# Making the low parts of late q and k on GpSimd instead of VectorE in a self-attention kernel

## The reference

```python
# x (8, 512, 512), cond (8, 512); W* (512, 512), b* (512); 16 heads of 32
Q  = split_heads(x @ Wq.T + bq);     K  = split_heads(x @ Wk.T + bk);   V = split_heads(x @ Wv.T + bv)
tQ = split_heads(tokens @ Wq.T + bq);  tK = split_heads(tokens @ Wk.T + bk)      # tokens = cond[:, None, :]
scores = einsum('bhqd,bhkd->bhqk', Q + tQ, K + tK) / sqrt(32)
out = einsum('bhqk,bhkd->bhqd', softmax(scores), V)
return x + out.transpose(0, 2, 1, 3).reshape(8, 512, 512)
```

## Time and profile before

| | |
|---|---|
| median of 3 runs | 639.27 us (638.93 to 641.06) |
| the profiled execution | 639.64 us, of it the span 637.8 us |
| TensorE, weight loads | 631.6 us busy (99%), 441.0 us (69%) |
| VectorE, ScalarE, GpSimd | 542.4 us (85%), 390.2 us (61%), 490.2 us (77%) |

### The profile page before, as it was taken

One profiled execution on the slowest core, in us unless ns is written; L12 is line 12 of the kernel. 1 busy time (PEld: TensorE's weight loads), 2 busy tenths in 40 slices (PEclk: granted clock), 3 DMA queues, 4 the chain that ended last, 5 costly groups with the idle time before them and its releaser, 6 DMA issues.

```text
span 637.8 us, 10063 instructions
## 1 busy us (share of the span) xinstructions
PE 631.6 (99%) x3528; PEld 441.0 (69%) x3528; DVE 542.4 (85%) x818; ACT 390.2 (61%) x684; POOL 490.2 (77%) x204
## 2 busy tenths in 40 slices
PE   8999999999999999999999999999999999999997
PEld 6777677666677666776666776666776666876642
DVE  6886888888888888888888888888888889998697
ACT  6366567666566565666665666665676655555773
POOL 6448877778877788877788777788777787767993
PEclk9999999999999999999999999999999999999999
DMA  8944435555335564434564344554354556555201
GB/s 254 272 102 119 104 103 127 121 152 145 97 102 122 138 152 126 107 105 119 149 151 116 105 115 118 151 151 106 105 126 118 151 127 158 134 120 130 76 31 67
DMA packets 48243, 80.83 MB, mean 127 GB/s; under 512 B 9545, under 2 KB 9801, under 8 KB 48073
## 3 DMA queue, kind: packets, MB, share of 16 engines
q1 hardware_dynamic: 47837, 80.04, 48.7%
q10 hardware_dynamic: 356, 0.16, 0.1%
HBM read 19.95 MB, written 8.39 MB: 44 GB/s over the span
## 4 chain that ended last, share of the span: by engine, by line
PE 97%; DVE 1%; DMA 1%; SPq 0%; POOLq 0%; ACT 0%; issue 0%
PE bank L354 27%; PE bank L447 19%; PE bank L429 18%; PE bank L467 18%; PE bank L402 14%; DVE bank L751 1%; PE bank L498 1%; DMA Pt<-xT 1%; PE bank L475 0%; PE bank L379 0%; DVE Xl L720 0%; POOLq L82 0%; ACT Xh L594 0%; DVE rr L789 0%; DVE rr L800 0%
## 5 line engine op out<-in xcount | busy, mean ns | idle before, releaser
L647 ACT ACTIVATE Pt<-bank 128x512 f32<-128x512 f32 x512 | 301.0, 599 | 222.1 <-PE bank L447 156.7
L751 DVE TENSOR_REDUCE mf<-bank 128x1 f32<-128x512 f32 x496 | 330.9, 684 | 60.7 <-PE bank L429 59.7
L959 POOL TENSOR_TENSOR A<-A,Pt 128x2048 f32<-128x2048 f32 x59 | 271.3, 4598 | 4.6
L429 PE MATMUL bank<-Ks,Qs 128*128 128x512 f32 x496 | 194.3, 392 | 0.1
L447 PE MATMUL bank<-Qs,Ks 128*128 128x512 f32 x496 | 194.0, 398 | 0.3 <-DVE bank L751 0.3
L959 POOL TENSOR_TENSOR A<-Pt 128x2048 f32<-128x2048 f32 x30 | 138.4, 4612 | 25.5 <-DVE part_sums L776 22.1
L447 PEld LDWEIGHTS bank<-Qs,Ks 128*128 128x128 f32 x496 | 92.6, 188 | 46.9 <-ACT Pt L647 23.3
L467 PE MATMUL bank<-Pt,V 128*32 128x512 f32 x1024 | 119.0, 596 | 0.0
L429 PEld LDWEIGHTS bank<-Ks,Qs 128*128 128x128 f32 x496 | 93.0, 188 | 21.7 <-DVE bank L751 1.8
L354 PE MATMUL bank<-Xh,Wh 128*128 128x512 f32 x256 | 100.1, 391 | 0.4 <-ACT Xh L594 0.3
L354 PE MATMUL bank<-Xl,Wh 128*128 128x512 f32 x256 | 99.8, 390 | 0.3 <-DVE Xl L720 0.3
(11 more groups left out here) (74 smaller groups left out, 392.6 us busy)
## 6 DMA issues: line engine op xcount, KB each, us to landing
Qs<-hi SPq DMA_DIRECT2D x60, 256.0 KB
Ks<-hi SPq DMA_DIRECT2D x60, 256.0 KB, 4.0
Qs<-lo SPq DMA_DIRECT2D x30, 256.0 KB
Ks<-lo SPq DMA_DIRECT2D x30, 256.0 KB, 3.9
xr<-xT SPq DMA_DIRECT2D x28, 256.0 KB, 2.7
res<-xT SPq DMA_DIRECT2D x28, 256.0 KB, 2.9
outT<-ot SPq DMA_DIRECT2D x28, 256.0 KB, 3.6
Qs<-mt SPq DMA_DIRECT2D x122, 4.0 KB
```

What stands on the lines that cost most here:

```text
L429: e.matmul(MXB[u % 2][:, :], q[:, j, qc * P:(qc + 1) * P], k[:, j, :], start=True, stop=True).then_inc(t_mx, 1)
L647: e.activation(exponentials(g)[:, kc, j, :], st_bank(u)[:, :], ACT.Exp, scale=SCALE).then_inc(a_e, 1)
L751: e.reduce_max(to[:, 4 * j + qc:4 * j + qc + 1], MXB[u % 2][:, :], AXX).then_inc(v_mx, 1)
L959: e.tensor_tensor(sums, ex[:, 0, :, :] if kc == 1 else sums, ex[:, kc, :, :], ALU.add).then_inc(p_a, 1)
```

## The change

For groups 28 to 31, q and k, VectorE's `qk_lo` goes. ScalarE makes two activations of the bank: hi as before, and right behind it `whole`, bank + bias in float32, into a new buffer of 128 x 512 in SBUF, of which there is one. GpSimd subtracts hi from it (`qk_lo(i)` in the GpSimd program; i = 0 to 7 for q28, k28, q29 and so on) and signals p_lo. The bank is free in the ring after `whole` (a_f), the next `whole` may be written after GpSimd's subtraction of the one before (p_lo), and SP issues the copy of lo after p_lo. LATE_LO now gives, for each of the eight, a place in GpSimd's program: three places per group from group 25 on, ahead of `parts`, ahead of add(t, 1) and ahead of add(t, 2). By (1, 2, 3, 4, 6, 6, 8, 9), q28 stands ahead of add(25, 1), k28 ahead of add(25, 2), q29 ahead of parts(27), k29 ahead of add(26, 1), q30 and k30 ahead of parts(28), q31 ahead of add(27, 2) and k31 ahead of parts(29). The tables MAXIMA, LATE_PROJ and LATE_HI, a V copy, the value matmuls of group 28, the turn of the maxima of group 30 and the fourth score bank are placed anew.

```diff
--- before.py
+++ after.py
@@ -52,28 +52,28 @@
 
 
 EARLY = 7
-MAXIMA = ((1, 1, 1, 2, 1, 0, 2, 0, 1, 1, 1, 1, 2, 1, 0, 2),
-          (1, 1, 2, 1, 1, 1, 0, 2, 0, 2, 0, 2, 1, 1, 1, 1),
-          (1, 2, 2, 2, 0, 2, 0, 2, 0, 1, 1, 2, 1, 1, 1, 1),
-          (1, 1, 1, 1, 2, 0, 0, 1, 0, 2, 1, 1, 0, 2, 1, 1),
+MAXIMA = ((2, 0, 1, 2, 2, 0, 2, 0, 1, 1, 1, 1, 1, 1, 1, 2),
+          (1, 1, 2, 1, 1, 1, 0, 2, 0, 2, 0, 1, 1, 1, 2, 1),
+          (1, 1, 2, 2, 0, 2, 0, 2, 0, 1, 1, 2, 1, 1, 1, 1),
+          (1, 1, 1, 1, 2, 0, 0, 2, 0, 2, 1, 0, 1, 2, 1, 0),
           (1, 0, 1, 1, 1, 1, 1, 1, 0, 1, 1, 0, 1, 0, 0, 1),
           (1, 1, 0, 1, 1, 1, 0, 1, 1, 1, 0, 0, 0, 0, 0, 0))
 LATE = (("q", 28), ("k", 28), ("q", 29), ("k", 29), ("q", 30), ("k", 30), ("q", 31), ("k", 31),
         ("v", 28), ("v", 29), ("v", 30), ("v", 31))
-LATE_PROJ = ((1, 0, 3, 4, 4, 3, 3, 3, 0, 4, 1, 2, 3, 1, 2, 4),
-             (0, 0, 4, 0, 4, 4, 1, 5, 1, 3, 1, 3, 2, 1, 1, 1),
-             (2, 1, 5, 2, 4, 3, 2, 4, 4, 0, 3, 3, 1, 2, 1, 1),
-             (1, 0, 1, 2, 4, 1, 5, 3, 1, 3, 2, 1, 2, 3, 1, 1),
+LATE_PROJ = ((1, 1, 3, 4, 3, 3, 3, 1, 2, 4, 1, 2, 2, 1, 2, 4),
+             (0, 0, 5, 0, 5, 3, 0, 5, 1, 3, 1, 3, 2, 2, 3, 0),
+             (1, 0, 5, 1, 4, 4, 3, 4, 4, 1, 2, 3, 1, 2, 1, 2),
+             (0, 0, 1, 2, 4, 1, 5, 3, 0, 3, 2, 1, 2, 3, 1, 2),
              (1, 2, 1, 2, 0, 0, 0, 0, 0, 0, 0, 0, 0, 0, 0, 0))
-LATE_HI = ((4, 10), (15, 22), (31, 34), (39, 43))
-LATE_LO = ((5, 13), (16, 24), (32, 34), (40, 47))
-LATE_V = (50, 57, 67, 69)
-
-END_VALUES_AT = ((5, 13), (15,), (3, 7))
-END_TURN_AT = 5
+LATE_HI = ((4, 11), (16, 21), (27, 36), (39, 43))
+LATE_LO = (1, 2, 3, 4, 6, 6, 8, 9)
+LATE_V = (50, 57, 68, 69)
+
+END_VALUES_AT = ((5, 11), (15,), (3, 7))
+END_TURN_AT = 4
 END_SUMS_AT = 11
 POOL_ADDS = 2
-END_BANKS = ((1, 7, 3), (2, 12, 4))
+END_BANKS = ((1, 7, 3), (2, 14, 4))
 LAST_EARLY = (0, 1)
 LAST_ORDER = (0, 2, 3)
 
@@ -114,6 +114,7 @@
         res = sb("res", [P, S])
         rr = sb("rr", [P, S])
         ot = sb("ot", [P, S])
+        whole = sb("whole", [P, S])
         rc = sb("rc", [P, 16])
         mf = sb("mf", [P, 2, 16])
 
@@ -157,6 +158,7 @@
         p_mh = sem("p_mh")
         p_ml = sem("p_ml")
         p_a = sem("p_a")
+        p_lo = sem("p_lo")
 
 
         a_tc = sem("a_tc")
@@ -165,6 +167,7 @@
         a_x = sem("a_x")
         a_xc = sem("a_xc")
         a_hi = sem("a_hi")
+        a_f = sem("a_f")
         a_v = sem("a_v")
         a_e = sem("a_e")
 
@@ -214,7 +217,18 @@
 
         def freed(use):
             kind, g = use
-            return {"q": (v_lo, 2 * g + 1), "k": (v_lo, 2 * g + 2), "v": (a_v, g + 1)}[kind]
+            if kind == "v":
+                return a_v, g + 1
+            i = 2 * g + "qk".index(kind)
+            return (v_lo, i + 1) if g < G - 4 else (a_f, i - 2 * (G - 4) + 1)
+
+        def lo_made(e, qk, g):
+
+            i = 2 * g + qk + 1
+            if g < G - 4:
+                e.wait_ge(v_lo, i)
+            else:
+                e.wait_ge(p_lo, i - 2 * (G - 4))
 
 
         def v_bank():
@@ -622,6 +636,14 @@
                 e.activation(hi_part(qk, g), ring_bank(("qk"[qk], g))[:, :], ACT.Identity,
                              bias=b2[:, qk, c:c + 1]).then_inc(a_hi, 1)
 
+            def qk_whole(qk, g):
+                b, c = divmod(g, KC)
+                i = 2 * (g - (G - 4)) + qk
+                if i > 0:
+                    e.wait_ge(p_lo, i)
+                e.activation(whole[:, :], ring_bank(("qk"[qk], g))[:, :], ACT.Identity,
+                             bias=b2[:, qk, c:c + 1]).then_inc(a_f, 1)
+
             def v_copy(g):
                 b, c = divmod(g, KC)
                 e.wait_ge(t_vj, g + 1)
@@ -697,8 +719,12 @@
                         x_hi(g // KC + 1, g % KC)
                     if (g := projected(t, n, Q_HI_AT, [at[0] for at in LATE_HI])) is not None:
                         qk_hi(0, g)
+                        if g >= G - 4:
+                            qk_whole(0, g)
                     if (g := projected(t, n, K_HI_AT, [at[1] for at in LATE_HI])) is not None:
                         qk_hi(1, g)
+                        if g >= G - 4:
+                            qk_whole(1, g)
 
             g = G - 1
             b, c = divmod(g, KC)
@@ -874,7 +900,7 @@
                         u += 1
                     if t < G - 2 and (g := due(t, n, TURN_AT if t < G - 3 else END_TURN_AT, 1, 1)) is not None:
                         maxima_turned(g)
-                    if (g := projected(t, n, Q_LO_AT, [at[0] for at in LATE_LO])) is not None:
+                    if (g := projected(t, n, Q_LO_AT, ())) is not None:
                         qk_lo(0, g)
                     if t < G - 3 and (g := due(t, n, FINISH_AT[0], -2)) is not None:
                         sums_inverted(g, MXB[u % 2])
@@ -884,7 +910,7 @@
                         normalised(g)
                     if t < G - 3 and (g := due(t, n, FINISH_AT[3], -2)) is not None:
                         added(g)
-                    if (g := projected(t, n, K_LO_AT, [at[1] for at in LATE_LO])) is not None:
+                    if (g := projected(t, n, K_LO_AT, ())) is not None:
                         qk_lo(1, g)
                     if t < G - 3 and (g := due(t, n, SUMS_AT[0], -1)) is not None:
                         key_sums(g, 0)
@@ -928,6 +954,19 @@
                 e.wait_ge(a_x, KC + n + 1)
                 e.tensor_tensor(Xl[:, b % 2, kc, :], xr[:, n % 2, :], Xh[:, b % 2, kc, :].bitcast(F32),
                                 ALU.subtract).then_inc(p_x, 1)
+
+            def qk_lo(i):
+                g, qk = G - 4 + i // 2, i % 2
+                e.wait_ge(a_f, i + 1)
+                stack_landed(e, qk, g - 1)
+                e.tensor_tensor(lo_part(qk, g), whole[:, :], hi_part(qk, g).bitcast(F32),
+                                ALU.subtract).then_inc(p_lo, 1)
+
+            def late_lo(t, place):
+
+                for i, at in enumerate(LATE_LO):
+                    if at == 3 * (t - (G - EARLY)) + place:
+                        qk_lo(i)
 
             def parts(g):
                 e.wait_ge(v_mx, SLOTS * (g + 1))
@@ -987,8 +1026,11 @@
                 b, kc = divmod(t + 3, KC)
                 if b + 1 < B:
                     x_lo(b + 1, kc)
+                late_lo(t, 0)
                 parts(t + 1)
+                late_lo(t, 1)
                 add(t, 1)
+                late_lo(t, 2)
                 add(t, 2)
             parts(G - 2)
             add(G - 4, 3)
@@ -1022,7 +1064,7 @@
                 for r in ((0, 1), (0, 2))[qk]:
                     e.dma_start(dst[r:96:3, :, :].bitcast(F32),
                                 hi_part(qk, g).bitcast(F32)).then_inc(d_st[sl][qk], 16)
-                e.wait_ge(v_lo, 2 * g + qk + 1)
+                lo_made(e, qk, g)
                 r = (2, 1)[qk]
                 e.dma_start(dst[r:96:3, :, :].bitcast(F32),
                             lo_part(qk, g).bitcast(F32)).then_inc(d_st[sl][qk], 16)
```

## The result

The changed kernel takes 641.12 us (median of 16 runs, 640.52 to 642.87), the kernel before 639.36 us in the runs beside it (16, 638.76 to 641.06): 1.0027 times, interval 1.0021 to 1.0034, or 1.76 us slower. The forecast was +1.1 us.

What follows compares the result with a forecast made beforehand. TensorE, busy 99% of the span, was taken as the bound. Terms 0 (removed) + 0.1 + 1.1 + 0 + 0 = +1.2 us, less half of a 0.2 counterweight, gave +1.1: 639.27 to 640.4 us, range 638.4 to 641.8.

Steps and rivals of the forecast that it cites:

- The main step: Group 27, slot 46: copy of k31 waits for lo(q31) behind add(27,1), delaying TensorE's score matmul; +1.1 us.
- The removal: Groups 28 to 31: taking eight subtractions, 5.9 us, off VectorE is worth 0 us, since none is on TensorE's path.
- The copy in slots 11 to 14 of group 25: hi(k28), its copy and two exponentials come together on ScalarE: +0.1 us, bounds 0 and 0.5.
- what is removed: Prediction's section on VectorE's eight subtractions: MAXIMA and LATE_PROJ totals are unchanged, so TensorE reaches group 29 with the same left over.
- The 0.1 us allowed for groups 29 and 30 as a counterweight: Groups 29 and 30, end placements and fourth score bank: taken as 0, bounds -0.2 and +0.2; half of 0.2 allowed as gain.
- No stall: Rival, chance 0.25: VectorE's key sums come early enough for add(27,1) to start by 567.5; only small terms left, 639.3 us.
- Faster: Rival, chance 0.06: VectorE enters groups 29 and 30 with a lead and TensorE's waits there go; 636.8 to 637.4 us.
- Late landing: Rival, chance 0.11: lo(q30) lands at 571.0, hi(q31) is 2.4 us late, slot 42's score matmul about 1.8; 641.1 us.
- GpSimd's reads held up: Rival, chance 0.05: VectorE holds lo(q31) through the shared SBUF read port by 0.68 to 1.23 us; 641.3 us.

Runs made afterwards that it cites:

- e1: Changed kernel with lo(q31) one place earlier on GpSimd, ahead of add(27,1): 640.29 us beside 639.31 for the kernel before, ratio 1.0019.
- e2: Changed kernel with two copy buffers, one for q and one for k, GpSimd's order kept: 640.04 us beside 639.31 for the kernel before, ratio 1.0007.
- e9: Changed kernel with the tables of the kernel before and two copy buffers: 639.38 us beside 639.27 for the kernel before, ratio 1.0002.
- e7: Changed kernel with two copy buffers, two group 25 table fixes, three maxima moved from group 30 into 26 to 28, three projections into group 29: ratio 1.0028.
- e5: Changed kernel with the tables of the kernel before, LATE_LO as changed, one copy buffer: 641.87 us beside 639.22 for the kernel before, ratio 1.0040.

## Why the prediction was right, and where its size was short

**The main step held to a tenth.** Forecast: add(27,1) at 568.68, lo(q31) done at 574.66, ScalarE standing 1.2 us, the exponential at 575.28, the score matmul of slot 46 at 575.94, 1.1 us lost. Found: 568.70, 574.56, 1.15 us, 575.18, 575.82, 0.99 + 0.11 us. e1 and e2 take away the place and the buffer separately, and the wait goes both times. That the clock times agree so well is partly luck: in this execution group 25 begins 0.83 us earlier than in the one before (516.66 and 517.49), and the 0.97 us by which groups 25 and 26 are longer make up for it. The lengths, 1.15 us of ScalarE and 0.99 us of TensorE, do not depend on that.

**The removal was worth nothing, as said**: in e9, with the buffer mended, no group is more than 0.04 us shorter than before (groups 29 and 30 take 12.04 and 11.00 us, before 12.08 and 10.99). The reason given (VectorE ends no wait of TensorE in groups 25 to 28, and the tables bring no maximum out of groups 29 and 30) stands. One reading in it was too short: the table behind the earlier trace rows does put 1.7 us of waits of weight loads for the totals (four) down to VectorE, but the starts there follow each other as their neighbours do, 0.41 us apart, so they are hidden. And e7 adds that group 30 did not get shorter when three maxima were taken out of it.

**What was short is 0.65 us.** Three terms of the sum:
- The copy in slots 11 to 14 of group 25 was put at 0.1 us, bounds 0 and 0.5; it measured 0.34 (0.23 of wait and 0.11 in the step behind it). The mechanism was the one named; the 0.1 had no working behind it, and the 0.11 was counted for the copy of k31 and not here.
- In "what is removed" I added up the rows of MAXIMA and concluded that TensorE has the same work. The sum is right, the order was not looked at: two maxima in slot 0 instead of one and one cost 0.15 us, since the second needs the reduction two before it, and VectorE takes 0.68 us each.
- The 0.1 us allowed for groups 29 and 30 as a counterweight was not there: 39.53 us before, 39.58 after. The wait at slot 12 of group 30 fell from 0.49 to 0.10 us by the starts, and slot 13 got one of 0.30: the prediction had argued that another wait would take its place, but had it at slot 15.

Group 27 holds another 0.2 us. It is there in e1 and e2 too (20.43 and 20.45 us, where 20.43 less one matmul would be 20.20) and not with the old tables and two buffers (e9), so it belongs to the new tables. Two starts hold 0.13 of it: the projection at 556.54 comes 0.27 us behind the matmul ahead, and the first value matmul, at 557.42, comes 0.42 instead of 0.33. Both stand behind maxima whose weight loads came late, the first after 0.19 us of waiting for VectorE: the order of the maxima once more. The rest is 0.001 us per step over some 70 steps.

**The rivals.** "No stall" failed: the key sums were 0.4 us sooner (the second ends at 568.49), not 1.2; and add(27,1) has a second condition that I had passed over, the exponential of slot 39, which ended at 568.56 (568.73 before) and released it in the end: sooner key sums alone could never have removed the stall. "Faster" failed at its own point: VectorE had no backlog at group 29, and stood idle for 2.0 us waiting for a maximum in that stretch (2.3 before). "Late landing" did not come: hi(q31) started at 568.46 behind its exponential. "GpSimd's reads held up" did not come either: the eight subtractions lie between 1.283 and 1.298 us with VectorE beside them; VectorE's reductions ran through the whole of lo(q31), for one. "Perfetto Trace Analysis" of the Trainium skill (Optimizing Scalar/DVE Operations) warns of the shared SBUF read port; in this mix of instructions no run here shows a delay from it. The GPSIMD Engine Reference of the Trainium skill (4.1, engine selection) gives GpSimd as some 2 times slower for two-input work, which with VectorE's 0.742 us would be 1.48 us, an estimate; the trace has 1.290, the price that the x subtraction of the same shape gave.

## What to carry to other kernels

Before moving work off an engine, ask which wait of the bound engine that engine ends in that stretch; here none, and 5.9 us were worth nothing, while the added hand-over had a cost. With a single buffer between two engines, the producer's next write waits for the consumer's queue, so look at the longest instruction that stands ahead of the read: a 1.3 us subtraction behind a 4.6 us add on GpSimd stopped ScalarE and, through it, TensorE. And when a hand-made order is changed, check each slot, not the sums: two tables with the same totals differed by 0.5 us in group 25 (20.01 in e5, 20.48 in the changed kernel, with the same copies).

## What the runs showed that was not expected

- Most waits of TensorE in a queue of 0.23 us steps cost 0.11 us more than themselves, since the step behind them was 0.34 us: at 575.82, 534.51 and 517.38 alike. Each time the weight load of the matmul that waited started together with it. Where the load had started ahead, the extra step is missing: at 556.54 it was 0.23 us ahead, and the next step was 0.23. In groups 29 and 30 of the kernel before eight such steps, behind waits that are often under 0.05 us, add up to about 0.9 us.
- The spans of two profiles (1.1 us apart) understated the difference of the medians (1.76), because the first 40 us of an execution vary: the first score matmul starts between 37.5 and 40.3 us in the twelve profiles. Over groups 0 to 24 the runs agree within 0.25 us, and the late stretch alone gave 1.88.
- The tables of the kernel before hold VectorE's eight subtractions with no wait at all, at 92% busy; the new ones, laid out for a freer VectorE, lost 3 us and more when it had to make them, at the two sets of places that I tried.
